# Experts layer of an adaptive two-layer transformer: sends and second matrices in 32-row tiles, modulation on VectorE, tie added in PSUM, four batches staggered on TensorE

## The reference

```
h = layernorm(x) * (1 + cb) + sb            # cb, sb, gb: one row of 128 for each batch
grouped    = h.reshape(B, g, t, d)          # g = 8 groups of t = 32 tokens in a batch
logits     = einsum('bgtd,des->bgtes', grouped, controller) + tie      # 32 experts x 4 sets = 128 slots
perm       = (logits == max(logits, over the 32 tokens of a group))    # each slot takes one token of a group
dispatched = einsum('bgtd,bgtes->bgesd', grouped, perm)
inner      = relu(einsum('bgesd,desf->bgesf', dispatched, f1) + bias)  # f: 32 values
intermediate = einsum('bgesf,esfd->bgesd', inner, f2)
out        = einsum('bgesd,bgtes->bgtd', intermediate, perm)
x = x + gb * out
```

## Time and profile before

| | |
|---|---|
| median of three runs | 1505.26 us (1504.54 to 1508.08) |
| the profiled execution, its own time | 1505.55 us |
| span of its profile, first to last instruction | 1503.7 us |
| TensorE busy, share of the span | 1280.3 us, 85% |
| VectorE | 1139.2 us, 76% |
| ScalarE | 933.0 us, 62% |
| GpSimd | 550.9 us, 37% |
| mean granted TensorE clock | 0.942 of full |

### The profile page before, as it was taken

How to read it: one execution, slowest core, us unless ns; L and a number is a source line. 1 busy time by engine, 2 the same in 40 slices (tenths; PEclk the granted TensorE clock), 3 DMA queues, 4 the chain that set the end, 5 groups by cost and what they waited for, 6 DMA issues and landing times. The chain is left out here.

```text
span 1503.7 us, 37667 instructions
## 1 busy us (share of the span) xinstructions
PE 1280.3 (85%) x12442; PEld 827.7 (55%) x12442; DVE 1139.2 (76%) x3067; ACT 933.0 (62%) x1292; POOL 550.9 (37%) x771
## 2 busy tenths in 40 slices
PE   2688888888876877778758999999965999999998
PEld 1454455554533635454535555555533777777776
DVE  3799999999847575857568999999945677777763
ACT  0488888888872323232416888888864666766675
POOL 1233333333414131312113333333303656655653
PEclk6699999999998989998978999999986999999999
DMA  3311111111001010100020000000000000000000
GB/s 79 143 33 32 31 33 37 34 31 31 18 10 44 9 36 9 32 11 15 15 85 12 13 13 14 14 14 13 12 7 0 8 7 14 14 14 7 14 14 23
DMA packets 44734, 37.50 MB, mean 25 GB/s; under 512 B 5136, under 2 KB 43472, under 8 KB 44144
## 3 DMA queue, kind: packets, MB, share of 16 engines
q1 hardware_dynamic: 44656, 36.50, 8.3%
HBM read 32.14 MB, written 4.34 MB: 24 GB/s over the span
## 5 line engine op out<-in xcount | busy, mean ns | idle before, releaser
L1966 ACT ACTIVATE a_probs<-psum_all 128x1024 f32<-128x1024 f32 x256 | 248.1, 1022 | 86.8 <-PE psum_all L1881 86.8
L474 ACT ACTIVATE probs<-psum_all,biases 128x1024 f32<-128x1024 f32 x256 | 270.6, 1112 | 44.2 <-PE psum_all L385 43.4
L2354 PE MATMUL psum_all<-ffn_hi,weights_r 128*128 128x512 f32 x704 | 286.6, 407 | 8.2 <-POOL ffn_lo L2314 4.9
L2354 PE MATMUL psum_all<-ffn_lo,weights_r 128*128 128x512 f32 x704 | 280.5, 398 | 0.0
L2314 POOL TENSOR_TENSOR ffn_lo<-ffn_full,ffn_hi 128x512 fp32r<-128x512 f32 x144 | 189.7, 1326 | 126.7 <-ACT ffn_hi L2439 87.6
L2354 PEld LDWEIGHTS psum_all<-ffn_hi,weights_r 128*128 128x128 f32 x704 | 133.5, 190 | 50.0 <-DVE ffn_full L2569 8.7
L2354 PEld LDWEIGHTS psum_all<-ffn_lo,weights_r 128*128 128x128 f32 x704 | 134.2, 191 | 28.6
L398 PE MATMUL psum_all<-probs,vpad 128*32 128x257 f32 x2048 | 139.1, 389 | 0.3 <-ACT probs L474 0.3
L1895 PE MATMUL psum_all<-a_probs,vpad 128*32 128x256 f32 x2048 | 137.9, 387 | 0.1
L2451 ACT ACTIVATE ffn_full<-psum_all,scales 128x512 f32<-128x512 f32 x128 | 88.2, 689 | 70.2 <-PE psum_all L2354 69.9
L2314 DVE TENSOR_TENSOR ffn_lo<-ffn_full,ffn_hi 128x512 fp32r<-128x512 f32 x64 | 55.0, 860 | 80.5 <-ACT ffn_hi L2454 80.5
(11 more groups left out here) (223 smaller groups left out, 2776.9 us busy)
## 6 DMA issues: line engine op xcount, KB each, us to landing
a_mod_gate<-modulation_table SPq DMA_DIRECT2D x64, 128.0 KB, 2.9
a_mod_norm<-modulation_table SPq DMA_DIRECT2D x32, 128.0 KB, 3.0
X<-in_x SPq DMA_DIRECT2D x32, 128.0 KB, 2.9
f<-in_f SPq DMA_DIRECT2D x2, 2048.0 KB, 10.0
e_mod_norm<-modulation_table SPq DMA_DIRECT2D x32, 128.0 KB, 2.9
out<-X SPq DMA_DIRECT2D x16, 256.0 KB, 2.3
e_gates<-modulation_table SPq DMA_DIRECT2D x32, 64.0 KB, 2.7
weights<-in_h SPq DMA_DIRECT2D x2, 1024.0 KB, 7.7
```

The lines of the kernel that those rows point to most:

```text
L474: nc.scalar.activation(probs[:, c % 4, :, :, 0:T].rearrange("p r k q -> p (r k) q"), SC[c % 2].rearrange("p (a q) -> p a q", q=T), ACT.Tan ...
L1966: nc.scalar.activation(probs[:, c % 4, :, :, :].rearrange("p r k q -> p (r k q)"), SC[c % 2], ACT.Exp, scale=float(np.float32(1.0) / np.sq ...
L2354: ins = nc.tensor.matmul(dst, weights[:, w0:w0 + P], part[layer][:, k, :], start=first and i == 0, stop=last and i == len(parts) - 1)
```

## The change

In the routing, `send` becomes eight matmuls: for each tile and each group one with the group's 32 tokens contracted (32 rows of h as weights, 32 rows of e_taken with 128 columns moving), each group to its own bank (4 to 7). The masked copies and `own` go; e_taken is one copy of the transposed choice, on ScalarE (`taken_out`). The tie becomes a second matmul that adds to the logits in PSUM (a matrix with ones in row 0 only, by the tie row repeated for each group), and VectorE reads the logits from PSUM. The scale and shift go from POOL to VectorE: `centre` makes (x - mean) * scale, `modulate` makes centred * root + shift. There are eight buffers of h and of e_mod_norm. TensorE's step is turn(k), score(k-1), turn_taken(k-2), send(k-3). At a chunk's start TensorE waits for the last e_delta of the chunk before send(0) only.

In the middle there is one relu on ScalarE for each round, and `second_matrices` makes 32 matmuls of 64 columns in a round, each with one set's 32 rows contracted, each set to its own bank: banks 4 to 7 in even rounds, 0 to 3 in odd ones. All first matrices come first. `results_out` copies two banks per engine and round.

In the hand-back e_givenT has four buffers, TensorE takes tiles in pairs, and the addition to X goes to POOL (`residual`); VectorE keeps the multiplication (`gate`).

```diff
-HB = 4
+HB = 8
...
 def load(c, j):
     wait(sp, mod_loaded, c * (16 * CB_) + 16 * j)
-    wait(sp, h_done, c * CB_ + (j - 1))
-    sp.dma_start(mod_norm[j % 2][:, :, :], rows_of(c, j, ROW_CB0, 2)).then_inc(mod_loaded, 16)
+    wait(sp, h_done, count(c, j - HB + 1))
+    sp.dma_start(mod_norm[j % HB][:, :, :], rows_of(c, j, ROW_CB0, 2)).then_inc(mod_loaded, 16)
...
 def score(c, j):
     wait(pe, hT_done, count(c, j + 1))
-    wait(pe, logits_done, c * CB_ + j)
-    nc.tensor.matmul(bank[1][:, 0:T], ctrl[:, :], hT[:, :], start=True, stop=True).then_inc(logits_psum, 1)
+    wait(pe, takenT_done, count(c, j))
+    nc.tensor.matmul(bank[1][:, 0:T], ctrl[:, :], hT[j % 2][:, :], start=True, stop=False)
+    nc.tensor.matmul(bank[1][:, 0:T], first_row[:, :], tie[:, :].unsqueeze(1).broadcast_to([P, T // GT, GT]),
+                     start=False, stop=True).then_inc(logits_psum, 1)
...
 def send(c, j):
     wait(pe, taken_done, count(c, j + 1))
     wait(pe, sent_done, count(c, j))
+    if j == 0:
+        wait(pe, delta_done, c * CB_)
     for t in range(TT):
-        last = nc.tensor.matmul(bank[3 + t], h[j % HB][:, t, :], taken[:, t, :, :].rearrange("p g s -> p (g s)"), ...)
+        for g in range(TG):
+            rows = slice(GT * g, GT * (g + 1))
+            last = nc.tensor.matmul(bank[4 + g][:, t * SLOTS:(t + 1) * SLOTS], h[j % HB][rows, t, :], taken[rows, t, :], ...)
...
 def second_matrices(c, r):
-    wait(pe, relued_dve, c * ROUNDS + (r + 1))
-    wait(pe, relued_act, c * ROUNDS + (r + 1))
-    for pair in range(EB // 2):
-        n = r * (EB // 2) + pair
-        if n >= 4:
-            wait(pe, (given_dve, given_act)[n % 2], c * (GB_ // 2) + (n // 2 - 1))
-        for i in range(2):
-            e = 2 * pair + i
-            last = nc.tensor.matmul(bank[4 + n % 4][:, i * NS_ * CG:(i + 1) * NS_ * CG], f2[:, r * EB + e, :],
-                                    relued[r % 2][:, e, :, :].rearrange("p s g -> p (s g)"), start=True, stop=True)
-        last.then_inc(given_psum, 1)
+    wait(pe, relued_done, c * ROUNDS + (r + 1))
+    if r == 1:
+        wait(pe, inner_done, c * ROUNDS + ROUNDS)
+    if r >= 2:
+        wait(pe, given_dve, c * ROUNDS + (r - 1))
+        wait(pe, given_act, c * ROUNDS + (r - 1))
+    for e in range(EB):
+        for s in range(NS_):
+            rows = slice(NF * s, NF * (s + 1))
+            last = nc.tensor.matmul(given_banks(r)[s][:, e * CG:(e + 1) * CG], f2[rows, r * EB + e, :],
+                                    relued[r][rows, e, :], start=True, stop=True)
+    last.then_inc(given_psum, 1)
...
-    for k in range(CB_ + 2):
+    for k in range(CB_ + 3):
         if k < CB_:
             turn(c, k)
-        if k < CB_:
-            score(c, k)
         if 0 <= k - 1 < CB_:
-            turn_taken(c, k - 1)
-        if k >= 2:
-            send(c, k - 2)
-    first_matrices(c, 0)
-    first_matrices(c, 1)
+            score(c, k - 1)
+        if 0 <= k - 2 < CB_:
+            turn_taken(c, k - 2)
+        if 0 <= k - 3:
+            send(c, k - 3)
     for r in range(ROUNDS):
-        if r + 2 < ROUNDS:
-            first_matrices(c, r + 2)
+        first_matrices(c, r)
+    for r in range(ROUNDS):
         second_matrices(c, r)
-    turn_back(c, 0)
-    for q in range(TB_):
-        if q + 1 < TB_:
-            turn_back(c, q + 1)
+    for q in range(4):
+        turn_back(c, q)
+    for q in range(0, TB_, 2):
         hand_back(c, q)
+        hand_back(c, q + 1)
+        if q + 4 < TB_:
+            turn_back(c, q + 4)
+            turn_back(c, q + 5)
...
+def results_out(eng, copy, done, c, r, s0):
+    wait(eng, given_psum, c * ROUNDS + (r + 1))
+    for s in (s0, s0 + 1):
+        slots = slice(r * EB * NS_ + s, (r + 1) * EB * NS_, NS_)
+        last = copy(given[:, :, slots].rearrange("p g e -> p e g"), given_banks(r)[s].rearrange("p (e g) -> p e g", g=CG))
+    last.then_inc(done, 1)
...
 @block.scalar
+def taken_out(j):
+    wait(act, taken_psum, count(c, j + 1))
+    wait(act, sent_psum, count(c, j))
+    nc.scalar.copy(taken[:, :, :].rearrange("p t s -> p (t s)"), bank[2][:, 0:T]).then_inc(taken_done, 1)
...
+def relu(r):
+    wait(act, inner_done, c * ROUNDS + (r + 1))
+    nc.scalar.activation(relued[r][:, :, :], inner[r % 2][:, :, :], ACT.Relu).then_inc(relued_done, 1)
...
 @block.vector
+def centre(c, j):
+    wait(dve, moments_done, count(c, j))
...
+    wait(dve, moments_done, count(c, j + 1))
+    wait(dve, mod_loaded, c * (16 * CB_) + 16 * (j + 1))
+    wait(dve, h_done, count(c, j))
+    for t in range(TT):
+        last = nc.vector.scalar_tensor_tensor(out=centred[:, t, :], in0=tile(c, j, t), scalar=moments[:, t, 0:1],
+                                              in1=mod_norm[j % HB][:, 0, :], op0=ALU.subtract, op1=ALU.mult)
+    last.then_inc(centred_done, 1)
+def modulate(c, j):
+    wait(dve, centred_done, count(c, j + 1))
+    wait(dve, rstd_done, count(c, j + 1))
+    wait(dve, sent_psum, count(c, j - HB + 1))
+    for t in range(TT):
+        last = nc.vector.scalar_tensor_tensor(out=h[j % HB][:, t, :], in0=centred[:, t, :], scalar=rstd[:, t:t + 1],
+                                              in1=mod_norm[j % HB][:, 1, :], op0=ALU.mult, op1=ALU.add)
+    last.then_inc(h_done, 1)
...
     for k in range(CB_ + 1):
         if k + 2 < CB_:
-            moments_of(c, k + 2)
-        if k < CB_:
-            choose(k)
+            modulate(c, k + 2)
+        if k + 3 < CB_:
+            centre(c, k + 3)
         if k >= 1:
-            own_groups(k - 1)
-        if k + 2 < CB_:
-            standardise(c, k + 2)
-    relu(0)
+            choose(k - 1)
+    if not is_last(c):
+        centre(c, CB_)
     for r in range(ROUNDS):
-        if r + 1 < ROUNDS:
-            relu(r + 1)
-        for n in range(r * (EB // 2), (r + 1) * (EB // 2)):
-            if n % 2 == 0:
-                results_out(dve, nc.vector.tensor_copy, given_dve, c, n)
+        add_bias(r)
         if not is_last(c) and r < 2:
-            moments_of(c, CB_ + r)
-            standardise(c, CB_ + r)
+            modulate(c, CB_ + r)
+            centre(c, CB_ + r + 1)
+    for r in range(ROUNDS):
+        results_out(dve, nc.vector.tensor_copy, given_dve, c, r, 0)
     for q in range(0, TB_, 2):
         turned_out(dve, nc.vector.tensor_copy, givenT_dve, c, q)
-        if q >= 2:
-            residual(q // 2 - 1)
-    residual(CB_ - 1)
+        if q >= 4:
+            gate(q // 2 - 2)
+    gate(CB_ - 2)
+    gate(CB_ - 1)
```

More of the change, by code:

```diff
@@ L799, in experts_0 @@
     X, ident, minus_half, eps = (sbuf[k] for k in ("X", "ident", "minus_half", "eps"))
-    ctrl, f1, f2, bias, tie, own = sbuf["experts"]
-    mod_norm = [sb(f"mod_norm{i}", [P, 2, D]) for i in range(2)]
+    ctrl, f1, f2, bias, tie, first_row = sbuf["experts"]
+    mod_norm = [sb(f"mod_norm{i}", [P, 2, D]) for i in range(HB)]
     gates = sb("gates", [P, CB_, D])
@@ L862, in chunk @@
                 if not is_last(c):
-                    load(c, CB_)
-                    load(c, CB_ + 1)
-            load(0, 0)
-            load(0, 1)
+                    for j in range(CB_, CB_ + HB):
+                        load(c, j)
+            for j in range(HB):
+                load(0, j)
             chunk(0)
@@ L1122, in choose @@
                                             best[:, :].unsqueeze(2).broadcast_to([P, T // GT, GT]), ALU.is_equal).then_inc(takenT_done, 1)
-                def own_groups(j):
-                    wait(dve, taken_psum, count(c, j + 1))
-                    wait(dve, sent_psum, count(c, j))
-                    for t in range(TT):
-                        last = nc.vector.tensor_tensor(taken[:, t, :, :], bank[2][:, t * P:(t + 1) * P].unsqueeze(1).broadcast_to([P, TG, SLOTS]),
-                                                       own[:, :].unsqueeze(2).broadcast_to([P, TG, SLOTS]), ALU.mult)
-                    last.then_inc(taken_done, 1)
@@ L1176, in chunk @@
+                if not is_last(c):
+                    centre(c, CB_)
+                for r in range(ROUNDS):
+                    add_bias(r)
+                    if not is_last(c) and r < 2:
+                        modulate(c, CB_ + r)
+                        centre(c, CB_ + r + 1)
+                for r in range(ROUNDS):
+                    results_out(dve, nc.vector.tensor_copy, given_dve, c, r, 0)
+                wait(dve, gates_loaded, c * (16 * CB_) + 16 * CB_)
                 for q in range(0, TB_, 2):
@@ L1189, in _ @@
             chunk(NCHUNK - 1)
+            wait(dve, x_done, B)
 SMALL_SCORE = 40.0
```

199 lines of the change are left out of this document (84 added, 115 removed).

## The result

| | before | after | forecast |
|---|---|---|---|
| median | 1505.12 us (1504.54 to 1508.08) | 1461.99 us (1457.48 to 1462.17) | 1428.0 (1405 to 1462) |
| ratio to before, 95% interval | | 0.970 (0.968 to 0.9725) | 0.949 |
| profiled execution, and its span | 1505.55, 1503.7 | 1462.04, 1460.0 | |
| mean granted clock | 0.942 | 0.916 | |
| four routings | 167.0 us | 134.2 us | 133.3 |

The change gained 43 us of the 77 that the sum promised. The first term came out; the middles cost 22.4 us more than forecast and the hand-backs 8.7. (Some 32 of the 33.8 us between the profiled execution and the sum lie in these stages. The rest is 1.1 us more from the start of the next part of the program to the end, 0.6 because this part starts 1.9 instead of 1.3 us after the last hand-back, and 0.2 outside the span. It was not followed up.)

The account below looks back on a forecast made before the run. Routing was taken as bound by two full loops, VectorE alone and send, copies and score, at 4.08 us a step. Gains of 33.6 (routing), 31.4 (middle) and 12.3 (hand-back) sum to 77.3: 1505.3 to 1428 us, range 1405 to 1462.

Parts of the forecast that it names:

- The first term: Gain in the four routings: 33.6 us, down to 133.3 us.
- the likeliest case: The forecast itself, 1428 us, own range 1408 to 1442, chance 0.56.
- Routing: Four routings of 133.3 us; VectorE's step 2.94 us for 4.08, TensorE's 2.4 at full clock.
- the forecast wait behind modulate and centre: Start of chunks 1 to 3: norms fill VectorE's queue until 4.5 us ahead of choose(0), which ends at 5.4.
- Row tiles overlap: Second matrices and sends: 32-row loads run four at once; a round of second matrices takes 1.9 us.
- Both rivals on the loads: Row-tile loads in series: 1533 us, chance 0.07; overlap only across matmuls in program order: 1457 us, chance 0.12.
- The hand-back's step: Tiles in pairs on TensorE: 1.59 us a pair instead of 1.88, gaining 12.3 us in four chunks.
- The copies out: Second matrices' results, written as single words 512 bytes apart, copied at 0.685 us each on VectorE.
- a rival at 0.12: Scattered writes cost double: copies out 1.4 us each on VectorE, about 3.8 more per middle, 1443 us; chance 0.12.
- The clock in the middle: Half clock possible only after TensorE's 2.1 us wait for the last add_bias; second(1) then ends at 11.8, not 10.0.
- The rival on the clock: Clock stays half through routing and after the middle's wait: about +7 us per chunk, 1456 us; chance 0.10.
- The first matrices: Start of the middle: all first matrices take 3.9 us, 256 records at 14.7 ns.

Follow-up runs that it names:

- Experiment 5: On top of experiment 4, VectorE's queue has choose(k-1) before modulate(k+2) and centre(k+3); 1427.11 us, ratio 0.9485.
- experiment 4: Changed kernel with the edits of Experiment 1 and of experiment 2, third form, together; 1435.81 us, ratio 0.9533.
- experiment 2: Changed kernel with copies out of the second matrices writing runs instead of single scattered words, in three forms; 1451.33, 1455.27 and 1449.25 us.
- experiment 2, first form: Changed kernel with each copy out writing 512 words side by side, slots in another order in e_given; 1451.33 us, ratio 0.9638.
- experiment 2, third form: Changed kernel with slots numbered set by set, so copies write runs of eight words and read PSUM at a stride; 1449.25 us, ratio 0.9635.
- Experiment 1: Changed kernel with each second-matrix matmul also multiplying the next expert's 64 columns, 128 under the same load; 1450.88 us, ratio 0.9651.
- experiments 3: Changed kernel with matmuls nobody reads filling TensorE's waits at the end of the routing; 1462.51 us, ratio 0.9712.
- experiment 8: Experiment 5's kernel with matmuls nobody reads filling TensorE's waits at the end of the routing; 1424.48 us, ratio 0.9475.

## Why the prediction was right, and where it was wrong

The sign and most single prices were right; the size was not. The time lies 0.01 us inside the range's upper end, 1462, where the rivals stood, and not in the likeliest case's own range (1408 to 1442). That it lies inside is luck: the range reached so far for rivals that did not come as they were written.

- **Routing: right**, 134.2 us for 133.3, but partly by terms that cancel. VectorE's step is 2.81 for 2.94 forecast; TensorE's 2.34 for 2.4. TensorE waits 4.16 us for choose(0) at the start of chunk 1, which is the forecast wait behind modulate and centre. In that chunk choose(0) ended at 6.5 and not 5.4, and the tail behind choose(7) took 6.55 and not 5.2, while choose(0) to choose(7) took 17.4 and not 19.0, since only 3.4 us there were at half clock, for some 10 forecast. Experiment 5 shows that choosing first was worth 8.7 us by the medians; what it gained lies in three of the four chunks.
- **Row tiles overlap: right.** Sixty-four records with their loads take 2.01 us, for 1.9 taken; the bounds were 3.4 in program order and 6.8 in series. Both rivals on the loads fell. The prediction had worked out 3.4 as the least if the strict order of start and end that the Trainium skill states ("TensorE: Matmul & The Clock Gate", the section on packing small matmuls) holds with a matmul's two records next to each other. The 2.01 us disagree with that working, for row tiles of float32 as for column tiles. That the order itself is broken is not shown: a record of the profile does not name its tile.
- **The hand-back's step: right**, 1.60 us a pair for 1.59. The stage is 8.7 us over because its start lies in the stretch at half clock that the middle leaves behind, 3.64 us for sixteen transposes that take 2.2 at full clock. Behind middles that keep their clock in the second matrices it measured 51.9 for 50.8 (experiment 4).
- **The copies out: the step that failed first.** I wrote "No row has that write" and took 0.685 us, with 1.4 as a rival at 0.12. It measured 1.29, 1.03 of it VectorE's own price. ScalarE's half took 1.30, for 0.59 in runs. Repaired copies gained 11 and 13 us in the first and third form of experiment 2, near the 15 of the rival, and part of that came by the clock: half level lay over 36 and 26 us of their four middles, for 56 in the changed kernel. The row ahead of me was one in which each run is 32 bytes, and I priced by the number of words. The rule on 16-byte lines (the Trainium skill, "SBUF — State Buffer", "Door 1: The DMA port swizzle") has the direction right here, and runs of eight words cost nothing more, as it would have it; the size is from these runs.
- **The clock in the middle: the second step that failed, and in kind.** The prediction let the clock fall only where TensorE waits for the last add_bias. That wait came to 0.54 us and not 2.1, since the first matrices ended 2.3 us late, and the clock fell after it nevertheless, behind rounds in which TensorE had been busy 4.02 of 4.62 us. Experiment 1 shows that the streaming under each load has a part in this: twice the columns in the same 2.01 us, and the clock stays through the rounds. Experiment 2 shows that it is not the whole: with repaired copies and the same 64 columns the clock stayed in 7 middles of 12. Why it fell in the other 5 is open. The rival on the clock was at 1456 us, near the result, but its place was wrong: it had half clock through the routing, where it lay over 47 us, for 41 in the kernel before.
- **The first matrices: mis-sized.** 3.9 taken, 6.2 measured in chunk 1, 3.96 of it at half clock behind the waits of the tail. The prediction saw those waits (5.2 us in its sum of the tail) and not what they do to the stage behind. But the clock is not what decides: at full clock, in experiments 3 and 8, they took 5.0 to 6.7 us, and 4.0 to 4.4 without the gaps. The gaps end behind the arrival of instructions (experiment 8), a term that the sum put at nothing without a reason.

By the medians, of the 34 us between forecast and result some 26 went with the two repairs of experiment 4. Its profile is of an execution of 1438.0 us, 10.0 over the forecast: 3.2 in the routing (136.5 for 133.3), 2.1 in the middles and 1.1 in the hand-backs; the last 3.6 were not followed. Where exactly in the routing the half-clock stretches fall differs from kernel to kernel with the same instructions (134 to 140 us), and why is open.

## What to carry to other kernels

When a change makes a stage load-bound on TensorE, ask two things that the busy share does not show: how much is streamed under each load (more columns per load can be free and keep the clock), and whether results are still written in runs of some words (renumber the data if need be, rather than read the next weights at a stride). Count the instructions too: a stage of many small ones, once it is fast, may have to wait for them, and the rows show that only as idle time without a cause. Judge a rewritten stage together with the one behind it: here 7.6 of the 27.9 us by which the two repairs shortened middles and hand-backs lay in the hand-back, whose own instructions had been priced right.

## What the runs showed of the hardware

- Copies from PSUM of 128x512 float32: 0.68 us on VectorE and 0.59 on ScalarE into runs of 8 words or more, also when PSUM is read at a stride (experiment 2, third form); 1.03 on VectorE into single words 512 bytes apart; 1.29 and 1.30 when both engines do so at once.
- A 128x128 float32 weight load took 141 ns with the words side by side and 257 ns at a stride of 256 bytes.
- Float32 matmuls in 32-row tiles: 64 records in 2.01 us with 64 columns each and with 128.
- The granted clock fell from full to half after a stretch in which TensorE had been busy 4.02 of 4.62 us, in row tiles with 64 columns per load. With twice the columns per record and no more busy time (4.03 of 4.62 us) it stayed full. With 64 columns it fell in every middle whose copies both scattered and in 6 of 16 others.
- Idle time of TensorE without a visible cause, inside the matrices of the middle, ended in 41 cases of 42 from 1.2 to 1.6 us after a 16 KB packet of the instruction queue.
- Executions of one kernel spread over 1442 to 1459 us in one (experiment 2, first form) and 1434 to 1438 in another (experiment 4), whose second matrices keep the clock. That stretches at half clock make the spread is not shown: in experiment 2's third form the shortest and the longest execution (1445.9 and 1455.6 us) have the same mean clock, 0.924.
